# Second attention: where the next batch's value projection stands in TensorE's order

## The reference, cut to what matters

```
Q = relu(x @ Wq + bq);  K = relu(x @ Wk + bk);  V = relu(x @ Wv + bv)
scores = Q K^T / sqrt(8), causal mask;  attn = softmax(scores)
out = layernorm(attn @ V + x) * gamma + beta
```

## Time and profile before

| | |
|---|---|
| median of 3 runs | 1015.98 us (1015.56 to 1017.27) |
| the profiled execution, its own time | 1015.8 us |
| its span, first to last instruction | 1014.5 us |
| TensorE busy | 975.5 us, 96% |
| VectorE busy | 877.0 us, 86% |
| ScalarE busy | 832.0 us, 82% |
| GpSimd busy | 471.9 us, 47% |
| the second attention's loop | from about 707 us to 917 us of the span |

### The profile page before, as it was taken

How to read it: one execution, slowest core, us unless ns; L and a number is a source line. 1 busy time by engine, 2 the same in 40 slices (tenths; PEclk the granted TensorE clock), 3 DMA queues, 4 the chain that set the end, 5 groups by cost and what they waited for, 6 DMA issues and landing times.

```text
span 1014.5 us, 25982 instructions
## 1 busy us (share of the span) xinstructions
PE 975.5 (96%) x8953; PEld 787.7 (78%) x8953; DVE 877.0 (86%) x3718; ACT 832.0 (82%) x2232; POOL 471.9 (47%) x541
## 2 busy tenths in 40 slices
PE   7999999999999999999989999999999999999897
PEld 7898888988888989743268988888777777776566
DVE  6777989898989888799998999888989888896985
ACT  6888888888888888887797878876788888886786
POOL 2334545454545463606810102101888888893041
PEclk9999999999999999999999999999999999999999
DMA  9000000000000000000000000000000000000002
GB/s 380 31 2 2 2 2 2 2 2 2 2 2 2 2 2 2 2 1 1 0 1 1 1 1 1 1 11 11 23 23 23 24 23 22 23 3 1 1 2 84
DMA packets 8723, 18.31 MB, mean 18 GB/s; under 512 B 1296, under 2 KB 5648, under 8 KB 8208
## 3 DMA queue, kind: packets, MB, share of 16 engines
q1 hardware_dynamic: 8592, 16.65, 4.9%
HBM read 10.36 MB, written 2.10 MB: 12 GB/s over the span
## 4 chain that ended last, share of the span: by engine, by line
PE 78%; DVE 10%; ACT 6%; POOL 3%; issue 2%; DMA 0%; SPq 0%; DVEq 0%; ACTq 0%; POOLq 0%
PE PB L246 8%; PE PB L247 8%; PE PB L248 8%; PE PB L343 6%; PE PB L398 6%; PE PB L381 6%; PE PB L1812 5%; PE PB L1209 3%; PE PB L1211 3%; PE PB L1210 3%; PE PB L1784 3%; PE PB L1829 3%; PE PB L430 2%; PE PB L431 1%; PE PB L432 1%
## 5 line engine op out<-in xcount | busy, mean ns | idle before, releaser
L373 POOL TENSOR_TENSOR W<-W,small 128x512 f32<-128x512 f32 x128 | 138.7, 1083 | 215.1 <-DVE small L367 215.1
L362 ACT ACTIVATE W<-W,small 128x128 f32<-128x128 f32 x512 | 199.2, 392 | 29.1 <-DVE small L353 28.5
L246 PE MATMUL PB<-RR_s 128*128 128x256 f32 (+3 forms) x568 | 183.6, 323 | 4.9 <-DVE RR_s L264 3.4
L247 PE MATMUL PB<-RR_s 128*128 128x256 f32 (+3 forms) x568 | 176.0, 310 | 0.0
L248 PE MATMUL PB<-RR_s 128*128 128x256 f32 (+3 forms) x568 | 176.0, 310 | 0.0
L353 DVE CUSTOM_DVE_ANT_0 W<-PB,W 128x128 f32<-128x128 f32 x512 | 117.3, 284 | 38.9 <-PE PB L343 37.9
L1800 POOL TENSOR_TENSOR AR_s<-AR_s,small 128x512 f32<-128x512 f32 x128 | 129.5, 1041 | 14.4 <-DVE small L1793 14.3
L1183 ACT ACTIVATE AR_s<-PB,W 128x512 f32<-128x512 f32 (+2 forms) x160 | 100.5, 629 | 28.5 <-PE PB L248 22.8
L246 PEld LDWEIGHTS PB<-RR_s 128*128 128x128 f32 x568 | 107.7, 190 | 12.4 <-issue 4.2
L1197 DVE TENSOR_TENSOR RR_s<-AR_s,RR_s 128x512 fp32r<-128x512 f32 (+2 forms) x160 | 100.4, 637 | 17.2 <-ACT RR_s L1188 13.9
L1793 DVE CUSTOM_DVE_ANT_0 AR_s<-PB,W 128x128 f32<-128x128 f32 x512 | 111.0, 286 | 1.7
(11 more groups left out here) (387 smaller groups left out, 2440.9 us busy)
## 6 DMA issues: line engine op xcount, KB each, us to landing
W<-in_w SPq DMA_DIRECT2D x1, 5809.5 KB, 24.8
out<-XT SPq DMA_DIRECT2D x8, 256.0 KB, 2.3
W<-in_w SPq DMA_DIRECT2D x2, 512.0 KB, 5.1
W<-in_w SPq DMA_DIRECT2D x1, 1024.0 KB, 7.5
XF<-in_xT SPq DMA_DIRECT2D x1, 1024.0 KB, 10.9
W<-AR_s SPq DMA_DIRECT2D x16, 64.0 KB, 2.1
AR_s<-AR_s SPq DMA_DIRECT2D x16, 64.0 KB, 2.1
QS<-AR_s SPq DMA_DIRECT2D x12, 64.0 KB, 2.1
```

The costliest lines, as they stand in the source:

```text
L246: nc.tensor.matmul(out, lh, rh, start=True, stop=False)
L247: nc.tensor.matmul(out, ll, rh, start=False, stop=False)
L362: e = nc.scalar.activation(SS[r][:, hl], SS[r][:, hl], ACTF.Exp, bias=mx[r][:, h:h + 1], scale=-1.0, accum_out=rc[r][:, h:h + 1])
L373: nc.gpsimd.tensor_tensor(s3, s3, over(rc[r], 2, [128, 4, 128]), ALU.mult).then_inc(s_nrm, 1)
```

## The change

In TensorE's turn the value projection of batch q+1 and the weighted sums of batch q-2 change places. Both are in turns 2 to 30; in turns 0 and 1 there are no sums and in turn 31 there is no projection, so nothing changes there. Neither the tenants' order in either pair of banks nor any other engine's queue is changed, and no instruction is added or removed.

```
--- before.py
+++ after.py
@@ -2598,10 +2598,10 @@
                     pe_T5(4 * q - 4)
                     pe_T5(4 * q - 3)
                 steps_of(turned, q)
+                if q >= 2:
+                    pe_PV5(q - 2)
                 if q + 1 < NB5:
                     pe_v5(q + 1)
-                if q >= 2:
-                    pe_PV5(q - 2)
                 steps_of(projected, q)
                 steps_of(multiplied, q)
                 if q:
```

## The result

The changed kernel takes 1018.57 us (median of 13 runs, 1018.26 to 1020.31) against 1015.98 us (13 runs, 1015.40 to 1018.04): ratio 1.0024, 95% interval 1.0017 to 1.0032. It is 2.6 us slower where 2.8 to 2.9 had been forecast. The profiled execution took 1018.65 us around a span of 1017.3 us; before, 1015.8 around 1014.5.

What follows compares the result with a forecast made beforehand. TensorE, busy 96% of the span, was taken to set the loop's pace; 13 x 0.22 = 2.9 us, all else 0, on 1015.8 gave 1018.7, written as 1018.8 us (0.28% slower), range 1016.5 to 1020.8.

Steps and rivals of the forecast that it cites:

- Step 1: Sums in front, bare turns: ScalarE's copy holds them, so start unchanged, gap grows from 0.12 to 0.34 us, gain 0.
- bare turns: 16 turns (3, 4, 5, 7, 9 and so on to 29, 30) where the projection directly follows two groups of transposes.
- Step 2: Projection behind the sums, bare turns: it adds its own slot, 0.22 us each, high end 0.39 us.
- The argument about the exposed load: Behind the sums, the cost of leaving column tiles is already paid by the work that follows them, so 0.22 us holds.
- Step 3: Of 16 bare turns, later waits in turns 7, 29 and 31 swallow three losses; 13 pay, 13 x 0.22 = 2.9 us.
- Step 4: Padded turns: sums move up 0.22 us, no gap by a 0.09 us margin, cost 0, at most 1.2 us.
- padded turns: 13 turns (2, 6, 8, 10 and so on to 28) where tokens or gamma are turned in front of the projection.
- Step 5: Projection's readers, bare turns: result comes some 1.5 us later, but 0.7 us is left before VectorE reads it; cost 0.
- Rival A: Slots swallowed elsewhere, perhaps at every fourth turn's last transposes: no measurable change, leaving +1.5 us, 1017.3; chance 0.17.
- B: The 0.12 us before bare turns' sums is a full-array-to-column-tiles cost, so 16 gaps go: -1.9 us, 1013.9; chance 0.05.
- C: Projection costs 0.39 us behind column tiles and padded turns lose their 0.09 us: 6.3 us slower, 1022.1; chance 0.07.
- D: Sixteen longer idle spells drop TensorE's clock to 1.2 GHz for one turn: +6.6 us, 1025.3; chance 0.01.

Runs made afterwards that it cites:

- the kernel with the wait taken away: Against the kernel before, the weighted sums go between the two groups of transposes and get their bank there; 1050.3 us in one run.

## Why the prediction was right, point by point

**Step 1, the sums of bare turns do not start sooner: right.** 1.44 us behind the transposes before, 1.43 after, then with 0.34 us idle released by L1818. The kernel with the shorter projection and the one with the sums moved ahead show the cause from both sides.

**Step 2, 0.22 us for the slot: right.** Bare turns that pay grew by 0.22 or 0.23. The argument about the exposed load was right too: it moved from the 512-column work to the projection. The sign named for it was not: the chain was to show L1878 with 0.22 us still, and shows 0.42, with the 0.2 taken off its neighbour.

**Step 3, 13 turns pay and 3 don't: right.** The three later waits shrank by 0.28, 0.23 and 0.22 us. What GpSimd releases in turn 7 is the layer norm on ScalarE (L2007), which stands before the exponential; in turn 29 it is the exponential itself. Both are set outside TensorE's queue, which is all the step needs.

**Step 4, padded turns pay nothing: right,** by a separate kernel and by turns of unchanged length. **Step 5, the readers are not late: right;** VectorE never waited at L1883.

The sum, +2.9, compares with +2.85 in the traces over the loop and +2.8 in the span. The medians give +2.6 because before's runs are two groups and the change thins out the upper one: from its lower group alone (7 of 13 runs, median 1015.56) to the 12 lower runs after (median 1018.57) it is +3.0. That part was not foreseen. I took the median of before, 0.2 above the profiled execution, as spread, and wrote that the trace did not bear out a fall of the clock. In turn 7 that one execution happened to be without it, but the same trace has one behind the loop, where I had not looked (busy time by stretch, then the granted clock):

```profile
940.00:950.00 10.00, 7.40 (x46) 4.64 (x45) 9.54 (x62) 8.39 (x21) 0.00 (x0) 0.99 0.01 2
950.00:960.00 10.00, 7.81 (x55) 5.54 (x56) 8.59 (x52) 6.96 (x20) 0.00 (x0) 0.84 0.00 0
```

The upper end of the range has a small slip too: 1015.8 + 5.1 is 1020.9, not 1020.8.

Rival A fell with the turns of 7.00 us, B with the doubled projection, C with the unchanged padded turns and with bare turns that grew by 0.22 and not 0.39. D was wrong in its place, in the sign of what the change does to it, and in its price: the clock stays down for some 3 us and not for all the work of a turn, and costs 1.6 us and not 6.6.

## What to carry to other kernels

Work put in front of an instruction that waits is free up to the length of the wait; moved behind it, it costs its own slot, unless a later wait set by another engine swallows that. To price a slot, look for a turn of the loop that already lacks the work: turn 31 was such an experiment, ready in the trace. Before filling a gap with more work, ask which wait of the same turn has almost no slack left, and when a kernel's runs fall into two groups, take more than one trace.

## What the runs showed of the hardware that was not expected

After TensorE stood idle for about 1.9 us in turn 7 (busy 0.27 of 2 us from 758 to 760), its granted clock fell to 0.50 for about 3 us, in some executions and not in others with the same order in that turn: turn 8 took 8.39 us instead of 6.79, about 1.6 us, and before's two groups of runs lie about that far apart. With 0.80 us idle, one of 22 runs was in the upper group. The sixteen gaps of 0.34 us did not bring it down: in all traces with them the clock stays at 1.00 in the turns that follow, apart from turn 7's.

The fall is not tied to the end of the gap. It came 1.3 and 1.6 us after TensorE was busy again in two traces, with its return in another, and 0.7 us before it in the kernel with the wait taken away, whose gap in turn 7 lasts 3.00 us.

A fall need not cost anything. All 13 traces have one 37 to 41 us behind the scores of turn 31; in before's it follows gaps of 1.47 and 1.20 us, in a stretch where VectorE has 9.54 of 10 us and TensorE 7.40. It lasts about 3 us in some traces and about 7 in others. Yet from those scores to the end of the span all kernels but the one with the wait taken away take 103.4 to 104.0 us, whichever they had.

The Trainium skill, page "TensorE: Matmul & The Clock Gate", section "Part 1: The HAM clock gate (the "warmup" mystery)", says that the clock has two levels and that the monitor behind it runs free of the kernel's start. The traces agree with the two levels. If the monitor runs free, the same idle time may lower the clock in one execution and not in the next; the two groups of runs fit that, though no run here shows the monitor itself.
